# Graph attention on one core: the probabilities of three heads turned by VectorE's block transpose and a trip through DRAM

## What is computed

```python
q = (x @ Wq + bq).reshape(n, H, OUT_DIM)
k = (x @ Wk + bk).reshape(n, H, OUT_DIM)
v = (x @ Wv + bv).reshape(n, H, OUT_DIM)
alpha = einsum('ehc,ehc->eh', q[dst], k[src]) / sqrt(OUT_DIM)
ex = exp(alpha - segment_max(alpha, dst)[dst])
attn = ex / segment_sum(ex, dst)[dst]
agg = segment_sum(attn[:, :, None] * v[src], dst).reshape(n, HC)
x_attn = agg + x @ Wskip + bskip
h = x_attn @ Wlin + blin + x_attn[:, :OUT_DIM]      # then normalised, a residual added, the lookup network
```

## Time and profile before

| | us |
|---|---|
| runs of the kernel before | 1083.4, 1084.77, 1086.65 |
| median | 1084.77 |
| the profiled execution, its own time | 1083.65 |
| span of the profiled execution | 1081.9 |
| PE busy | 1041.7 (96% of the span) |
| the first, second and third head, by windows | 204.21, 204.29, 204.24 |
| the last head with the tail | 207.05 |
| DVE busy | 543.3 (50%) |
| ACT busy | 334.7 (31%) |

### The profile page before, as it was taken

One profiled execution on the slowest core, in us unless ns is written; L12 is line 12 of the kernel. 1 busy time (PEld: TensorE's weight loads), 2 busy tenths in 40 slices (PEclk: granted clock), 3 DMA queues, 4 the chain that ended last, 5 costly groups with the idle time before them and its releaser, 6 DMA issues.

```text
span 1081.9 us, 13730 instructions
## 1 busy us (share of the span) xinstructions
PE 1041.7 (96%) x5213; PEld 852.2 (79%) x5213; DVE 543.3 (50%) x1349; ACT 334.7 (31%) x529; POOL 89.7 (8%) x256
## 2 busy tenths in 40 slices
PE   7999999999999999999999999999999999999993
PEld 5777777778888888888888888888888888877872
DVE  6998996532443443234434422443443235557676
ACT  4445644111332232122223211322222123334342
POOL 2120201000000000000000000000000000324244
PEclk9999999999999999999999999999999999999996
DMA  9745644300200020002002000200020001010110
GB/s 323 262 181 192 248 162 146 157 1 1 78 1 1 1 79 1 1 1 79 1 1 78 1 2 1 78 1 1 1 78 1 1 1 44 30 30 21 39 37 37
DMA packets 14972, 64.75 MB, mean 60 GB/s; under 512 B 1840, under 2 KB 2218, under 8 KB 11580
## 3 DMA queue, kind: packets, MB, share of 16 engines
q1 hardware_dynamic: 10300, 47.07, 12.5%
q0 software_dynamic: 4608, 16.78, 3.9%
HBM read 44.51 MB, written 19.34 MB: 59 GB/s over the span
## 4 chain that ended last, share of the span: by engine, by line
PE 78%; DVE 8%; issue 7%; ACT 3%; DMA 3%; POOL 1%; SPq 0%; DVEq 0%; ACTq 0%
PE ps_o L1239 9%; PE ps_o L1241 9%; PE ps_o L1240 9%; PE ps_r L1239 7%; PE ps_r L1240 7%; PE ps_r L1241 7%; PE ps_s L1241 7%; PE ps_s L1239 7%; PE ps_s L1240 6%; PE ps_t L1455 4%; PE ps_t L1239 1%; PE ps_t L1241 1%; PE ps_t L1240 1%; DVE onehot_src L836 1%; DMA early<-in_Wv 1%
## 5 line engine op out<-in xcount | busy, mean ns | idle before, releaser
L1239 PE MATMUL ps_s<-xT_hi,tT 128*128 128x512 f32 (+1 forms) x480 | 174.5, 364 | 0.0
L1241 PE MATMUL ps_s<-xT_hi,tT 128*128 128x512 f32 (+1 forms) x480 | 169.4, 353 | 0.0
L1240 PE MATMUL ps_s<-xT_lo,tT 128*128 128x512 f32 (+1 forms) x480 | 169.0, 352 | 0.0
L1239 PE MATMUL ps_o<-y,pT 128*128 128x512 f32 x400 | 156.5, 391 | 0.0
L1241 PE MATMUL ps_o<-y,pT 128*128 128x512 f32 x400 | 156.1, 390 | 0.0
L1240 PE MATMUL ps_o<-y,pT 128*128 128x512 f32 x400 | 155.9, 390 | 0.0
L734 ACT ACTIVATE pT<-ps_t 128x512 fp32r<-128x512 f32 (+1 forms) x120 | 58.8, 525 | 221.9 <-PE ps_t L1455 221.9
L791 ACT ACTIVATE prob<-prob,nbias 128x1250 f32<-128x1250 f32 x40 | 53.7, 1342 | 236.2 <-DVE nbias L1202 236.2
L1194 DVE CUSTOM_DVE_ANT_0 prob<-ps_s,maskb 128x1250 f32<-128x1250 f32 x40 | 58.2, 1455 | 118.4 <-issue 118.3
L1075 DVE TENSOR_TENSOR pT<-ps_t,pT 128x512 fp32r<-128x512 f32 (+1 forms) x120 | 68.5, 598 | 87.1 <-ACT pT L734 87.1
L1241 PEld LDWEIGHTS ps_s<-xT_hi,tT 128*128 128x128 f32 x480 | 90.8, 189 | 13.5
(11 more groups left out here) (241 smaller groups left out, 1728.4 us busy)
## 6 DMA issues: line engine op xcount, KB each, us to landing
products<-prod_parts POOLq DMA_DIRECT2D x32, 512.0 KB, 3.9
gbuf<-products SPq DMA_DIRECT2D x4, 2048.0 KB, 7.7
mbuf<-products SPq DMA_DIRECT2D x4, 2048.0 KB, 7.9
stage<-in_Wskip SPq DMA_DIRECT2D x4, 1024.0 KB, 5.7
stage<-in_Wq SPq DMA_DIRECT2D x3, 1024.0 KB, 10.0
stage<-in_Wk SPq DMA_DIRECT2D x3, 1024.0 KB, 6.6
stage<-in_Wv SPq DMA_DIRECT2D x3, 1024.0 KB, 4.7
stage<-in_Wlin SPq DMA_DIRECT2D x3, 1024.0 KB, 5.2
```

The source lines that it names most:

```text
L1239: nc.tensor.matmul(out_, a[0], b[0], start=start, stop=False)
L1240: nc.tensor.matmul(out_, a[0], b[1], start=False, stop=False)
L1241: return nc.tensor.matmul(out_, a[1], b[0], start=False, stop=stop)
```

## The change

For the first three heads the ten PE transposes of each tile are gone. In their place DVE transposes all 32x32 blocks of the 128x1280 tile in one instruction (`turn`), from `prob[0]` into `prob[1]`, with the blocks already grouped by the partitions that they shall land in. SP stores each quarter of the partitions by a DMA of its own into a DRAM tensor `regrouped` (32 partitions, four runs of 1280 bytes each), waits for all four, and loads the tile back by a fifth DMA into `whole`, 5120 bytes for each partition (`regroup`). ACT and DVE then form `pT` from `whole` in two halves (`whole_high`, `whole_low`) and not from PSUM in three groups. The last head keeps PE's transposes. The buffers change with that: both `prob` are wider by 30 columns, the probabilities of the first three heads always go to `prob[0]`, and the ring of `tT` has five slots where it had six, so the two jobs of step 1 move to step 2, in the last head too. On DVE the low parts of the `ps_r` jobs now stand behind the product with `count`, the inverse and the transpose. SP issues the two large loads of a head between these transfers. The counters of `outputs` count halves.

```diff
-T_SLOT = [2, 3, 4, 5, 0, 1, 2, 3, 4, 5]
-T_SLOTS = 6
+T_SLOT = [1, 2, 3, 4, 0, 1, 2, 3, 0, 1]
+T_SLOTS = 5
+HALVES = [(0, NS // 2), (NS // 2, NS)]
...
-        t_jobs = {1: [(1, 0), (1, 1)], 3: [(1, 2), (1, 3)], 5: [(2, 0)], 7: [(2, 1)]}
+        t_jobs = {2: [(1, 0), (1, 1)], 3: [(1, 2), (1, 3)], 5: [(2, 0)], 7: [(2, 1)]}
...
+            def regroup(h, d):
+
+                n = NT * h + d
+                sp.wait_ge(turned, n + 1)
+                to = regrouped[d % 2].rearrange("(r a) q c -> q a r c", r=Q)
+                for q in range(Q):
+                    part = prob[1][QR * q:QR * q + QR, :].rearrange("p (r c) -> p r c", r=Q)
+                    sp.dma_start(to[q], part).then_inc(stored, 16)
+                sp.wait_ge(stored, 16 * Q * (n + 1))
+                sp.wait_ge(pt_free, 2 * n + 1)
+                sp.dma_start(whole[:].rearrange("p q k b -> p (q k b)"),
+                             regrouped[d % 2].rearrange("p q c -> p (q c)")).then_inc(whole_in, 16)
+
             with sp.Fori(0, H - 1) as h:
-                sp.wait_ge(rot_done, rot(h, LAST_Y + 1))
-                sp.dma_start(mbuf[:].bitcast(F32), mats[bass.ds(2 * h + 3, 1)][0]).then_inc(m_in, 16)
-                sp.wait_ge(rot_done, rot(h, LAST_T + 1))
-                sp.dma_start(gbuf[:].bitcast(F32), mats[bass.ds(2 * h + 2, 1)][0]).then_inc(g_in, 16)
+                for d in range(NT):
+                    regroup(h, d)
+                    if d == 1:
+                        sp.wait_ge(rot_done, rot(h, LAST_Y + 1))
+                        sp.dma_start(mbuf[:].bitcast(F32), mats[bass.ds(2 * h + 3, 1)][0]).then_inc(m_in, 16)
+                    if d == 7:
+                        sp.wait_ge(rot_done, rot(h, LAST_T + 1))
+                        sp.dma_start(gbuf[:].bitcast(F32), mats[bass.ds(2 * h + 2, 1)][0]).then_inc(g_in, 16)
...
+            def whole_high(h, d):
+
+                act.wait_ge(whole_in, 16 * (NT * h + d + 1))
+                for g, (a, b) in enumerate(HALVES):
+                    act.wait_ge(out_ps, 2 * (NT * h + d) + g + 1)
+                    nc.scalar.activation(pT[:, 0, a:b, :].rearrange("p k (q b) -> p k q b", q=Q),
+                                         whole[:, :, a:b, :].rearrange("p q k b -> p k q b"), ACT.Copy).then_inc(pt_hi, 1)
...
+            def turn(h, d):
+
+                if d:
+                    dve.wait_ge(stored, 16 * Q * (NT * h + d))
+                blocks = prob[0][:].rearrange("p (k r b) -> p r k b", r=Q, b=QR)
+                nc.vector.transpose(prob[1][:].rearrange("p (r k b) -> p r k b", r=Q, b=QR),
+                                    blocks).then_inc(turned, 1)
...
+            def whole_low(h, d):
+
+                for g, (a, b) in enumerate(HALVES):
+                    dve.wait_ge(pt_hi, 2 * (NT * h + d) + g + 1)
+                    nc.vector.tensor_tensor(pT[:, 1, a:b, :].rearrange("p k (q b) -> p k q b", q=Q),
+                                            whole[:, :, a:b, :].rearrange("p q k b -> p k q b"),
+                                            pT[:, 0, a:b, :].rearrange("p k (q b) -> p k q b", q=Q).bitcast(F32),
+                                            ALU.subtract).then_inc(pt_free, 1)
...
-                    for local, g, half in side_fills(last, d):
-                        rotating_lo(h, local, "t", (g, half, h if g else h + 1), last)
...
+                    if not last and d < NT:
+                        turn(h, d)
+                    for local, g, half in side_fills(last, d):
+                        rotating_lo(h, local, "t", (g, half, h if g else h + 1), last)
...
-            def outputs(h, d, hid=None):
+            def outputs(h, d, last, hid=None):
                 n = NT * h + d
-                pe.wait_ge(pt_free, 3 * n + 3)
+                pe.wait_ge(pt_free, PE_TURNED + 3 * d + 3 if last else 2 * n + 2)
...
-                    if 0 <= d - 1 < NT:
+                    if last and 0 <= d - 1 < NT:
                         transposes(h, d - 1, [0, 1])
```

More of the change, by code:

```diff
@@ L49 @@
 XW = NS * P
+Q = 4
+QR = P // Q
+HALVES = [(0, NS // 2), (NS // 2, NS)]
+PE_TURNED = 2 * NT * (H - 1)
 LAST_ROWS = N - (NS - 1) * P
@@ L259, in graph_layer @@
         maskb = put("maskb", [P, N], BF16)
-        prob = [put(f"prob{i}", [P, N], F32) for i in range(2)]
+        prob = [put(f"prob{i}", [P, XW], F32) for i in range(2)]
+        whole = put("whole", [P, Q, NS, QR], F32)
         assert at[0] <= nc.sbuf_usable_end, at[0] - nc.sbuf_usable_end
@@ L422, in t_bank, with at_prob @@
             return ps_r[:, local % 2, T_GROUPS[g][1] * P * j:T_GROUPS[g][1] * P * j + T_COLS[g][1]]
+        def at_prob(last, d):
+            return prob[d % 2 if last else 0][0:R, 0:N]
         def g0_row(h):
@@ L784, in head @@
                         feat_copy(d - 5)
-                    if 0 <= d - 2 < NT:
-                        pt_high(h, d - 2, [2])
+                    if last and 0 <= d - 2 < NT:
+                        pt_high(d - 2, [2])
                     if last and 0 <= d - 3 < NT:
@@ L790, in head @@
                         act.wait_ge(nbias_ready, n + 1)
-                        nc.scalar.activation(prob[d % 2][0:R, :], prob[d % 2][0:R, :], ACT.Exp, scale=SCALE,
+                        nc.scalar.activation(at_prob(last, d), at_prob(last, d), ACT.Exp, scale=SCALE,
                                              bias=nbias[0:R, d:d + 1]).then_inc(exp_done, 1)
@@ L803, in head @@
                         scale_rows(d - 4)
-                    if 0 <= d - 1 < NT:
-                        pt_high(h, d - 1, [0, 1])
+                    if last and 0 <= d - 1 < NT:
+                        pt_high(d - 1, [0, 1])
+                    if not last and 0 <= d - 1 < NT:
+                        whole_high(h, d - 1)
             with act.Fori(0, H - 1) as h:
@@ L1182, in head @@
                     n = NT * h + d
-                    if 0 <= d - 2 < NT:
-                        pt_low(h, d - 2, [2])
+                    if last and 0 <= d - 2 < NT:
+                        pt_low(d - 2, [2])
                     if last and 0 <= d - 3 < NT:
@@ L1192, in head @@
                         dve.wait_ge(mask_ready, n + 1)
+                        if not last and d:
+                            dve.wait_ge(turned, n)
                         nc.vector.memset(total[:], 0.0)
-                        nc.vector.tensor_tensor_reduce(prob[d % 2][0:R, :], ps_s[0:R, 0:N], maskb[0:R, :], 1.0,
+                        nc.vector.tensor_tensor_reduce(at_prob(last, d), ps_s[0:R, 0:N], maskb[0:R, :], 1.0,
                                                        -0.1 * MASKED, ALU.subtract, ALU.max,
@@ L1205, in head @@
                         results(d - 5)
-                    for local, g, half in side_fills(last, d):
-                        rotating_lo(h, local, "t", (g, half, h if g else h + 1), last)
                     if d < NT:
                         dve.wait_ge(exp_done, n + 1)
-                        nc.vector.tensor_tensor_reduce(prob[d % 2][0:R, :], prob[d % 2][0:R, :],
+                        nc.vector.tensor_tensor_reduce(at_prob(last, d), at_prob(last, d),
                                                        count[0:R, d, 0:N], 1.0, 0.0, ALU.mult, ALU.add,
@@ L1225, in head @@
                         add_out(h, d - 2, last)
-                    if 0 <= d - 1 < NT:
-                        pt_low(h, d - 1, [0, 1])
+                    if last and 0 <= d - 1 < NT:
+                        pt_low(d - 1, [0, 1])
+                    if not last and 0 <= d - 1 < NT:
+                        whole_low(h, d - 1)
                     if last and d == 2:
@@ L1361, in _ @@
             for t in range(NT):
-                nc.tensor.transpose(ps_s[0:R, 2 * H * t:2 * H * t + 2 * H], cd_rows[:, R * t:R * t + R],
-                                    ident[0:2 * H, 0:2 * H])
+                ins = nc.tensor.transpose(ps_s[0:R, 2 * H * t:2 * H * t + 2 * H], cd_rows[:, R * t:R * t + R],
+                                          ident[0:2 * H, 0:2 * H])
+                if t < len(HALVES):
+                    ins.then_inc(out_ps, 1)
             nc.tensor.matmul(ps_cc, ones[:, 0:R], bsum[:], start=True, stop=True).then_inc(cd_done, 1)
@@ L1482, in outputs @@
                 for t in range(NS):
-                    if t == PT_GROUPS[2][0]:
-                        pe.wait_ge(pt_free, 3 * n + 4)
+                    if last and t == PT_GROUPS[2][0]:
+                        pe.wait_ge(pt_free, PE_TURNED + 3 * d + 4)
+                    if not last and t == HALVES[1][0]:
+                        pe.wait_ge(pt_free, 2 * n + 3)
                     if t == 3 and hid is not None:
@@ L1524, in head @@
                     if 2 <= d < NT + 2:
-                        outputs(h, d - 2, d - 5 if last and d >= NT else None)
-                    if 0 <= d - 1 < NT:
+                        outputs(h, d - 2, last, d - 5 if last and d >= NT else None)
+                    if last and 0 <= d - 1 < NT:
```

23 lines of the change are left out of this document (13 added, 10 removed).

## The result

The changed kernel takes 1042.57 us (median of 4 runs, 1041.71 to 1043.38), the kernel before 1085.06 (1083.4 to 1086.65) on the same chips: a ratio of 0.9608, with a 95% interval of 0.9592 to 0.9625. Forecast were 1042 us, with a range of 1038 to 1046.

What follows compares the result with a forecast made beforehand. PE's own time was taken to bound the three changed heads. Removing 35.1 + 3.8 + 3.8 = 42.7 us from the profiled 1083.65 gave 1040.95, or 1042 us at the runs' median, range 1038 to 1046.

Steps and rivals of the forecast that it cites:

- 35.1 us for the transposes: PE's queue, first three heads: transposes and slower starts behind them cost 1.17 us a tile, 35.1 us for 30 tiles.
- The two seams of 0.12 us: PE, behind each of a tile's two transpose groups: the next matmuls start late, counted as 0.12 us each.
- 3.8 and 3.8 us for the stalls: PE waits that go: value tile after step 1's jobs (3 x 1.0 + 0.8), last two transposes at head's end (three times 1.27).
- DVE's part: DVE after a tile's scores: transpose 1.5 us, all work done at +9.3 us, so the transpose costs PE nothing.
- cover: Plain step: 4.2 us of DVE time before PE's next scores end at +13.6 us and need DVE again.
- slack: Step 7, tightest place: low parts of `tT` end at +7.8 us, `scores(8)` asks at +9.5, 1.7 us left.
- the rule of 5.7 us: Plain step: a DVE transpose over 5.7 us lengthens each step by the rest; below that it costs PE nothing.
- The round trip: Tile's store to DRAM and load back: two legs of about 4 us, taken as 8 us, bounds 5.2 to 15.4.
- a round trip of up to 18.6 us is hidden: From transpose to outputs two steps on: no loss up to 18.6 us; beyond, 0.5 us a tile per us.
- first rival: Long round trip makes outputs wait for `whole`: slower than before from 21.4 us, 1123 us at 24; chance 4%.
- the prediction's own upper bound for the trip: Store and load through DRAM: two legs of at most 7.7 us each, 15.4 us, held to be hidden.
- More DMA beside the matmuls: PE's matmuls beside the added DMA traffic: no slowing, charged 0, as output blocks took 6.82 us with or without a load.

Runs made afterwards that it cites:

- the dead transposes: Changed kernel with ten unread, unwaited PE transposes a tile put back at their old places in the first three heads: 1075.59 us.
- The second transpose: Changed kernel with DVE's transpose done twice in a row in the first three heads: 1041.91 us.
- At 17 us: Changed kernel with two extra DRAM to DRAM copies of each tile between store and load, each waited for: 1108.23 us.
- Without the passage: Changed kernel without the DMAs through DRAM and their waits, `whole` a constant, the first three heads' output left out: 1042.06 us.
- the ring alone: Kernel before with only the five-slot ring and the jobs of step 1 moved to step 2, PE's transposes kept: 1080.92 us.
- four transposes in a row: Changed kernel with DVE's transpose done four times in a row in the first three heads: 1063.98 us.

## Why the prediction was right, and where it was not

**The bound.** A head was PE's own time, and is so now (190.44 of 190.44 us). Leaving PE's queue was therefore worth its full length, as the dead transposes show.

**35.1 us for the transposes: right.** The dead transposes cost 11.67 us in the first head, 34.9 in all. The two seams of 0.12 us belong to it: without them the count would have been 28. That of one transpose's own row (273 ns) would have been 82.

**3.8 and 3.8 us for the stalls: right for the change as a whole.** The three heads lost 13.96, 13.85 and 13.99 us, 41.8 in all, where 11.7 + 1.0 + 1.27 = 13.97 each were due. The two terms do not stand alone, though: with PE's transposes still there the ring gives 0.6 us a head and not 1.0, because two of them then wait for DVE's low part of `pT`. The 4.1 us by which its median moved are no confirmation of the 3.8. In the last head I counted 0.8 and it was 0.6: moving the jobs to step 2 brought a wait of 0.20 for `pT` there, which has no counterpart before.

**DVE's part: right in its numbers.** 1.51 us for the transpose (1.5), the list done at +9.24 us behind the scores' end of 548.29 (9.3), cover 4.57 (4.2; its own numbers, 13.6 - 9.3, give 4.3). The second transpose was free, as the slack of 1.8 us in step 7 (1.7) says. Where it breaks down first was told half right: the price for a much longer transpose came from steps 1, 2, 3 and 7, which the text had gone through as tight, and from the head's end, and not from the plain step from which the rule of 5.7 us was made.

**The round trip: the size was right (8.25 for 8), the limit wrong.** The step that failed is the one that takes a tile's own latency, from the transpose to the outputs two steps on, as the only condition: "a round trip of up to 18.6 us is hidden", and 0.5 us a tile for each us behind that. It left out that SP issues and waits for each tile in order, so that the queue's own 4.3 us a leg have to fit in one step and not in two; that the steps 0 and 1 are only 9.5 us; and that the stores of a tile that catches up with the load before them take 6.2 us and behind a large load 11.6. At 17 us the rule gives 1042.6, measured are 1108.23. The forecast did not suffer, since the queue was taken up for 4.7 us only; the first rival's threshold of 21.4 us did: the kernel is slower than before from somewhere between 12.5 and 17 us on. The trip could have been half as long again, then, but not twice as long, so the 4% for that rival rested on a margin that was not there: the prediction's own upper bound for the trip, 15.4 us, lies in the stretch in which the runs leave the outcome open. That bound of 7.7 us a leg was also taken from chosen rows: in the first stage of the kernel before a load of 1024 KB took up to 11.2 us from issue to landing. And the load does not always find DVE's low parts of the tile before done before its stores have landed: in steps with jobs it waits for them, at 514.10 by 3.4 us more than in a plain step. Neither cost anything here.

**More DMA beside the matmuls: nothing, as charged.** The DMA engines are busy for 0.30 of the second head instead of 0.06, and blocks of 30 outputs still take 6.82 us. Without the passage the time is the same to 0.5 us.

**The rule on transpositions.** The Trainium skill (VectorE: DVE Perf Modes, Rules for kernel authors) prefers TensorE for 128x128 transpositions. Here ten of them cost 1.17 us on an engine that was busy for 99% of a head, and 1.51 us on one that idles for 4.57 in a step even now; the measurement decides against the rule for this place, by 35 us. The factor of 19 for a strided DMA (the Trainium skill, VectorE: DVE Perf Modes, The three transpose paths) is stated there against the DMA's own transposition, which no run here measured, so the 74 us of the prediction, 19 times an ordinary store, are not what that section would give. The stores showed nothing of the kind: 640 KB in runs of 1280 bytes were stored in 4.3 us, all four stores with their issue.

**How near the sum came.** The profiled execution went from its own 1083.65 to 1043.38, 40.3 less and not 42.7. The heads gave 42.4; the stage ahead of them ended 2.2 us later (the first scores at 264.31 for 262.11), 0.7 of it there before 198.5 us and the rest by the dip of the clock in the last section. The medians are 42.5 apart. The executions of one kernel scatter by 1.7 to 3.3 us, so that the median hit the forecast to 0.6 us is in part luck; the heads, which hit it to 0.3 us, are the better witness.

## What to carry to other kernels

A step's list of work and its idle time on the helping engine say what a moved operation costs; on a queue that waits for its own transfers, first add up what it is occupied with for one tile, and hold that against one step, the shortest too, and over a whole head with the large loads in it, before following one tile's latency over several. Count a removed operation by the distances between starts of its neighbours, seams included, and put it back as dead work to check. Read an experiment's gain from the stretch of the trace that the edit touches and not only from the medians. A wait of 2 us in PE's queue cost nearly twice itself here (3.8 us), so a change of order that moves it away is worth trying even where the work stays.

## What the runs showed of the hardware that I had not expected

The granted clock fell behind small interruptions, and not in every execution. These are the windows of the changed kernel at the end of the stage ahead of the heads, and around its two waits of 2.16 us in the last head; then the first of them in the kernel before (the columns are those of the windows above; the granted clock is the third number from the end):

```profile
200.00:210.00 10.00, 10.00 (x34) 7.20 (x33) 5.76 (x17) 0.05 (x1) 0.00 (x0) 0.83 0.92 387
917.90:931.94 14.04, 11.88 (x58) 10.07 (x57) 7.55 (x25) 4.06 (x5) 3.13 (x10) 0.88 0.14 39
955.35:969.36 14.01, 11.85 (x58) 10.07 (x57) 7.56 (x25) 4.06 (x5) 3.12 (x9) 0.88 0.13 38
```

```profile
200.00:210.00 10.00, 10.00 (x43) 7.56 (x42) 6.05 (x18) 0.00 (x0) 0.00 (x0) 1.00 0.94 396
```

Behind 198.49 us PE ran 18 small matmuls, up to 201.57, and the clock fell just behind them (behind the same matmuls of the kernel before, at 197.82 to 200.90, it did not). At the lower of its two levels (1.2 for 2.4 GHz) matmuls of 512 columns start 0.427 us apart, not 0.227, and the dip costs some 1.7 us. It is missing from two of this study's thirteen profiles, that of before and that with two transposes (both 1.00 there), though none of the edits lies in that stretch; what decides whether it comes, the runs do not tell. In the last head the 24 narrow matmuls behind each wait take 3.9 us (up to 4.4 in other profiles) instead of 2.7 and the outputs behind them up to 7.34 instead of 6.82. Here too it is not in every execution: they take 2.78 us behind the second wait with the dead transposes and with four transposes in a row, and behind the first with the ring alone and with four tiles of the last head turned by DVE. There is a second source of scatter. PE's first matmul starts at 6.4 to 8.0 us in these thirteen profiles, and the small matmuls ahead of 200 us begin at 196.1 to 198.5, with no edit in that stretch. Three places with or without some 1.7 us, and a start that moves by up to 2.4, are enough for steps in the single times such as 1083.4 and 1086.65 of one and the same kernel; that they are all of the scatter is not shown.
